# Attention outputs divided by row sums from a ones column, with other hand-overs in the causal loops

## The reference, cut to what matters

```
L1:  S = (mixed q) k^T ; A = softmax(S) ; A = instance_norm(A over 256x256) * gamma + beta ; out = A v ; out @ projW + projb
L2:  S = q k^T / 4, causal ; A = softmax(S) ; out = A v ; t + out @ w_proj
L3:  the same with biases on q, k, v and on the output projection
```

## Time and profile before

| | before |
|---|---|
| median of 3 runs | 975.96 us (975.36 to 980.0) |
| the profiled execution | 974.61 us |
| its span | 972.6 us |
| mean granted clock of TensorE, of full speed | 0.923 |
| busy in the span: PE, weight loads, DVE, ACT, POOL | 83%, 65%, 79%, 65%, 20% |
| loop of l = 1 | about 104 to 326 us |
| loops of l = 2 and l = 3 | about 396 to 538 us, 653 to 796 us |

### The profile page before, as it was taken

How to read it: one execution, slowest core, us unless ns; L and a number is a source line. 1 busy time by engine, 2 the same in 40 slices (tenths; PEclk the granted TensorE clock), 3 DMA queues, 4 the chain that set the end, 5 groups by cost and what they waited for, 6 DMA issues and landing times.

```text
span 972.6 us, 19124 instructions
## 1 busy us (share of the span) xinstructions
PE 808.0 (83%) x5550; PEld 630.5 (65%) x5550; DVE 772.7 (79%) x2166; ACT 632.9 (65%) x1931; POOL 192.6 (20%) x234
## 2 busy tenths in 40 slices
PE   0876698889988755899999486559999997999997
PEld 0762576667766653678887356438778877677775
DVE  7327799999999835699999869938999994688886
ACT  0211587777877513689888564248889874688885
POOL 9001423443234110000000000010000010134344
PEclk9997899999999967799999798779999995799999
DMA  5000000000000091466666200035666650313130
GB/s 184 1 0 1 1 1 0 0 0 0 0 0 0 10 121 28 76 93 97 90 87 83 31 1 1 0 62 83 84 97 96 88 75 0 69 41 82 41 82 17
DMA packets 54355, 44.30 MB, mean 46 GB/s; under 512 B 28592, under 2 KB 42544, under 8 KB 54192
## 3 DMA queue, kind: packets, MB, share of 16 engines
q1 hardware_dynamic: 53872, 42.30, 27.9%
q0 software_dynamic: 448, 1.57, 0.6%
HBM read 12.33 MB, written 3.21 MB: 16 GB/s over the span
## 4 chain that ended last, share of the span: by engine, by line
PE 44%; DVE 12%; DMA 3%; issue 1%; ACT 1%; SPq 1%; POOL 0%; POOLq 0%; DVEq 0%; ACTq 0%
PE ps L839 7%; PE ps L850 6%; PE ps L720 6%; PE ps L624 6%; PE ps L670 5%; PE ps L661 3%; PE ps L626 3%; DVE chst L910 2%; DMA qk<-lo 2%; DVE on L929 2%; PE ps L551 1%; PE ps L634 1%; PE ps L635 1%; PE ps L647 1%; PE ps L826 1%
## 5 line engine op out<-in xcount | busy, mean ns | idle before, releaser
L419 ACT ACTIVATE ee<-ps,nmax 128x128 f32<-128x128 f32 (+1 forms) x588 | 249.5, 443 | 11.7 <-DVE nmax L990 9.9
L1031 DVE TENSOR_SCALAR ee<-ee,rrec 128x128 f32<-128x128 f32 (+1 forms) x588 | 174.8, 360 | 5.2
L720 PE MATMUL ps<-w,ee 128*128 128x128 f32 x960 | 137.0, 279 | 19.9 <-DVE ee L1031 19.9
L406 ACT ACTIVATE big<-ps 128x384 f32<-128x384 f32 (+1 forms) x224 | 113.5, 538 | 40.0 <-PE ps L720 39.4
L720 PEld LDWEIGHTS ps<-w,ee 128*128 128x128 f32 x960 | 103.9, 141 | 45.4 <-DVE ee L1031 35.6
L419 ACT ACTIVATION_READ_ACCUMULATOR ee<-ps,nmax 128x1 f32 x588 | 124.2, 211 | 0.0
L990 DVE TENSOR_REDUCE nmax<-ps 128x2 f32<-128x256 f32 x200 | 101.1, 545 | 18.0 <-PE ps L626 18.0
L624 PE MATMUL ps<-qk 128*128 128x128 f32 (+1 forms) x400 | 103.7, 348 | 13.4 <-DMA qk<-lo 10.8
L296 POOL TENSOR_TENSOR big<-qs,w 96x256 f32<-96x256 f32 x108 | 78.8, 761 | 144.4 <-ACT qs L429 144.4
L1234 DVE TENSOR_TENSOR hhl<-ee,hhl 128x512 fp32r<-128x512 f32 x96 | 81.7, 858 | 27.9 <-ACT hhl L525 26.2
L624 PEld LDWEIGHTS ps<-qk 128*128 128x128 f32 x400 | 79.8, 207 | 31.7 <-issue 17.9
(11 more groups left out here) (224 smaller groups left out, 1365.5 us busy)
## 6 DMA issues: line engine op xcount, KB each, us to landing
qk<-hi SPq DMA_DIRECT2D x36, 192.0 KB, 3.7
qk<-hi SPq DMA_DIRECT2D x72, 96.0 KB, 3.8
qk<-lo SPq DMA_DIRECT2D x36, 192.0 KB, 4.8
qk<-lo SPq DMA_DIRECT2D x72, 96.0 KB, 4.6
big<-moe_gate SPq DMA_DIRECT2D x8, 768.0 KB, 6.9
w<-w_in SPq DMA_DIRECT2D x1, 1831.5 KB, 12.9
xc<-x_in SPq DMA_DIRECT2D x4, 384.0 KB, 5.7
l_mix<-on SPq DMA_DIRECT2D x8, 192.0 KB, 6.6
```

What stands on the lines that cost most here:

```text
L406: nc.scalar.activation(et[:, h, 0:w], ps[:, 4 + hh, 0:w], ACT.Copy).then_inc(own(l, f"et{hh}"), 1)
L419: last = nc.scalar.activation(ee[:, ke, hh, qc, 0:w], src, ACT.Exp, bias=nmax[:, kp, hh, qc:qc + 1], accum_out=rsum[:, kp, hh, qc:qc + 1])
L720: last = nc.tensor.transpose(ps[:, 4 + hh, b * P:(b + 1) * P], ee[:, u, hh, qc, tc * P:(tc + 1) * P], ident)
L1031: last = V.tensor_scalar(v, v, rrec[:, kp, hh, qc:qc + 1], None, ALU.mult)
```

## The change

Four things are done at once.

1. Row sums. `normalise`, the accumulators of the exponentials and the sums of squares are gone. The values carry a column of ones, so that `weigh_values` gives the row sums with the outputs; the transposed outputs are then divided (`normalise_outputs`). In l = 1 the squares come from `bn_stats` of the undivided exponentials, put together behind the loop. Transposes wait for the exponentials themselves.
2. Causal outputs. They are transposed at u = 0, divided at u = 1, transposed back, copied by ACT (`oc`) and projected at u = 2 into bank 7, where before one step at u = 1 projected them in bank 6.
3. Causal queries and keys. Even heads stand in rows 0 to 63 of `qk`, odd heads in rows 64 to 127; a product reads 64 rows. `stack` issues each copy as two DMAs of 48 partitions: twelve for an image. `project_qk` moves ahead of the transposes of u = 0. The causal mask is added by one instruction of 256 columns for each head, not two of 128.
4. Order of ACT and DVE in the causal loops: both copies of probabilities of u = 0 are DVE's, with `keys` between them; `queries` stands right behind the output copy. `w1hl` gets a buffer of its own and is made behind the loop of l = 1, not behind that of l = 3.

```diff
@@ stack (SP)
                         for t, a0, a1 in moves:
-                            sp.dma_start(qk[t * HD:(t + 1) * HD, par, :, a0:a1, :].bitcast(F32),
-                                         part[:, a0:a1, :].bitcast(F32)).then_inc(own(l, "stacked"), 16)
+                            for hh in range(2):
+                                r0 = hh * 4 * HD + t * HD
+                                sp.dma_start(qk[r0:r0 + HD, par, :, a0:a1, :].bitcast(F32),
+                                             part[hh * (C // 2):(hh + 1) * (C // 2), a0:a1, :].bitcast(F32)).then_inc(own(l, "stacked"), 16)
@@ ACT, loop
+                        if l > 1 and u == 2:
+                            outputs_by_channel(l, i - 1)
                         exps(l, k + 1, (j + 1) % 2, (u + 1) % 3)
                         if u == 0:
                             outputs_to_sbuf(l, i - 1)
...
+                        if l > 1 and u == 0:
+                            queries(l, i + 2, par)
                         if l == 1 or u == 1:
                             copy_probs(l, k, 2 * u, 0)
-                        copy_probs(l, k, 2 * u + 1, 1)
-                        if l == 1 and u == 2:
...
+                        if l == 1 or u != 0:
+                            copy_probs(l, k, 2 * u + 1, 1)
@@ score_unit, causal
-                            mm(ps[:, 2 * kp + hh, qc * N:qc * N + w], qk[:, par, h, 0, qc * P:(qc + 1) * P], qk[:, par, h, 1, 0:w],
-                               start=True, stop=False)
-                            last = mm(ps[:, 2 * kp + hh, qc * N + qc * P:qc * N + (qc + 1) * P], identb[:, :], maskb[:, :], start=False, stop=True)
+                            r0 = hh * 4 * HD
+                            mm(ps[:, 2 * kp + hh, qc * N:qc * N + w], qk[r0:r0 + 4 * HD, par, u, 0, qc * P:(qc + 1) * P],
+                               qk[r0:r0 + 4 * HD, par, u, 1, 0:w], start=(qc == 0), stop=False)
+                    for hh in range(2):
+                        diag = ps[:, 2 * kp + hh, :].rearrange("p (b t) -> p b t", t=P)[:, 0::3, :]
+                        last = mm(diag, identb[:, :], mid_dim(maskb[:, :], 1, TPI), start=False, stop=True)
@@ PE, loop
+                        if l > 1 and u == 0:
+                            pe.wait_ge(sg("causal_added"), i + (LOOP_ADDS["added"] if l == 3 else 0) + START)
+                            project_qk(l, i + 2, par)
                         for hh in range(2):
-                            pe.wait_ge(*upto(l, "norm", 2 * k + (hh + 1)))
+                            if l > 1 and u == 2 and hh == 1:
+                                pe.wait_ge(*upto(l, "v_sb", i + 2))
+                                project_outputs(l, i - 1)
+                            pe.wait_ge(*upto(l, "exp", 2 * k + (hh + 1)))
...
@@ DVE
+            def normalise_outputs(l, i):
+                dve.wait_ge(*upto(l, "oq", i + 2))
+                src = ps[:, 6, 0:4 * C].rearrange("p (q h d) -> p q h d", q=TPI, d=2 * HD)
...
+                V.reciprocal(rec, src[:, :, :, HD]).then_inc(own(l, "orec"), 1)
+                dve.wait_ge(*upto(l, "orec", i + 2))
+                for q in range(TPI):
...
+                    last = V.tensor_tensor(dst.rearrange("p (h d) -> p h d", d=HD), src[:, q, :, 0:HD], last_dim(rec[:, q, :], HD), ALU.mult)
+                last.then_inc(own(l, "on" if l > 1 else "added"), 1)
@@ DVE, loop
+                        if l > 1 and u == 1:
+                            normalise_outputs(l, i - 1)
                         maxima(l, k + 2, j % 2)
...
+                        if l > 1 and u == 0:
+                            copy_probs(0)
+                            keys(l, i + 2)
+                            copy_probs(1)
+                        if l > 1 and u == 1:
+                            values(l, i + 1, npar)
+                        if l > 1 and u == 2:
+                            copy_probs(0)
+                            add_outputs(l, i - 1)
                         if l == 1:
-                            dve.wait_ge(sg("l1_norm"), 2 * k + 2)
...
+                            dve.wait_ge(sg("l1_exp"), 2 * k + 2)
+                            for hh in range(2):
+                                for q in range(TPI):
+                                    last = V.bn_stats(est[:, par, q, 2 * u + hh, :], ee[:, u, hh, q, :])
...
-                        normalise(l, k + 1, (j + 1) % 2, (u + 1) % 3)
...
@@ DVE, behind the loop of l = 1
+                    V.tensor_tensor(e4[:, :, :, 0], e4[:, :, :, 1], e4[:, :, :, 1], ALU.mult)
+                    link(V.tensor_tensor(r2, r1, r1, ALU.mult))
+                    link(V.scalar_tensor_tensor(out=e4[:, :, :, 0], in0=e4[:, :, :, 0], scalar=float(N // 2), in1=e4[:, :, :, 2], op0=ALU.mult, op1=ALU.add))
+                    link(V.tensor_tensor(e4[:, :, 0, 0], e4[:, :, 0, 0], e4[:, :, 1, 0], ALU.add))
+                    link(V.tensor_tensor(e4[:, :, 0, 0], e4[:, :, 0, 0], r2, ALU.mult))
+                    V.tensor_tensor(ssqa[:, :, :], e5[:, :, 0, :, 0, 0], e5[:, :, 1, :, 0, 0], ALU.add).then_inc(sg("l1_ssqa"), 1)
```

More of the change, by code:

```diff
@@ L418, in exps @@
                         src = ps[:, 2 * kp + hh, qc * N:qc * N + w]
[L419 to L420 removed]
+                        last = nc.scalar.activation(ee[:, ke, hh, qc, 0:w], src, ACT.Exp, bias=nmax[:, kp, hh, qc:qc + 1])
                     last.then_inc(own(l, "exp"), 1)
@@ L439, in outputs_to_sbuf, with outputs_by_channel @@
                 nc.scalar.activation(ots[0:C, :, :], ps[0:C, 6, :].rearrange("p (a t) -> p a t", a=2), ACT.Copy).then_inc(own(l, "ot"), 1)
+            def outputs_by_channel(l, i):
+                act.wait_ge(*upto(l, "oc_ps", i + 2))
+                nc.scalar.activation(oc[0:C, :], ps[0:C, 6, 0:N], ACT.Copy).then_inc(own(l, "oc"), 1)
             for l in (1, 2, 3):
@@ L1010, in add_outputs @@
             def add_outputs(l, i):
                 dve.wait_ge(*upto(l, "out_ps", i + 2))
-                if l == 1:
-                    for q in range(TPI):
-                        src = ps[:, 6, q * 2 * C:(q + 1) * 2 * C].rearrange("p (h d) -> p h d", d=2 * HD)[:, :, 0:HD]
-                        dst = on1[:, q, i + 1, :] if isinstance(i, int) else on1[:, q, bass.ds(i + 1, 1), :].rearrange("p a c -> p (a c)")
-                        last = V.tensor_copy(dst.rearrange("p (h d) -> p h d", d=HD), src)
-                else:
-                    tv = tok_all[:, bass.ds(i * TPI + TPI, TPI), :]
-                    last = V.tensor_tensor(tv, ps[:, 6, 0:TPI * C].rearrange("p (t c) -> p t c", c=C), tv, ALU.add)
@@ L1021, in add_outputs @@
-                last.then_inc(own(l, "added"), 1)
-            def normalise(l, k, kp, ke):
-                dve.wait_ge(*upto(l, "exp", 2 * k + 2))
-                V.reciprocal(rrec[:, kp, :, :], rsum[:, kp, :, :]).then_inc(own(l, "rec"), 1)
-                dve.wait_ge(*upto(l, "rec", k + 1))
-                for hh in range(2):
-                    for qc in range(TPI):
-                        v = ee[:, ke, hh, qc, 0:scores_cols(l, qc)]
-                        last = V.tensor_scalar(v, v, rrec[:, kp, hh, qc:qc + 1], None, ALU.mult)
-                    last.then_inc(own(l, "norm"), 1)
+                tv = tok_all[:, bass.ds(i * TPI + TPI, TPI), :]
@@ L1034, in _ @@
+                V.tensor_tensor(tv, ps[:, 7, 0:TPI * C].rearrange("p (t c) -> p t c", c=C), tv, ALU.add).then_inc(own(l, "added"), 1)
             for l in (1, 2, 3):
@@ L1052, in _ @@
                 keys(l, 1)
-                normalise(l, 0, 0, 0)
                 with dve.Fori(0, B // 2) as it:
@@ new lines, in _ @@
+                        if l == 1:
+                            dve.wait_ge(sg("l1_exp"), 2 * k + 2)
+                            for hh in range(2):
+                                for q in range(TPI):
+                                    last = V.bn_stats(est[:, par, q, 2 * u + hh, :], ee[:, u, hh, q, :])
+                            last.then_inc(sg("l1_est"), 1)
+                            if u == 2:
+                                dve.wait_ge(sg("l1_est"), TR0 + k + 1)
+                                V.tensor_copy(esta[:, bass.ds(i, 1)].rearrange("p a q h s -> p (a q h s)"),
+                                              est[:, par].rearrange("p q h s -> p (q h s)")).then_inc(sg("l1_esta"), 1)
@@ L1251, in get @@
         return np.asarray(inputs[name])
-    def heads_apart(w, bias=None):
-        out = np.zeros((P, 2, C), w.dtype)
-        out[:C].reshape(3, 2 * HD, 2, C)[:, :HD] = w.reshape(2, 3, HD, C).transpose(1, 2, 0, 3)
-        if bias is not None:
-            out[ONE, 0] = bias
-        return out
     def with_bias(w, bias):
```

159 lines of the change are left out of this document (87 added, 72 removed).

## The result

| | before | after |
|---|---|---|
| median of the runs side by side | 977.81 us (4 runs) | 994.66 us (991.95 to 997.23, 4 runs) |
| ratio, 95% interval | | 1.0173 [1.0131, 1.0215] |
| the profiled execution, its span | 974.61, 972.6 us | 993.85, 991.9 us |
| mean granted clock of TensorE | 0.923 | 0.908 |
| one image in the loop of l = 1 | 13.50 us | 11.81 us |

What follows compares the result with a forecast made beforehand. Bounds: PE's wait for DVE in l = 1; PE and the circle of `hi` together in the causal loops. 974.6 - 29.6 + 2.4 + 2 x (27.0 + 1.9 + 2.1) = 1009.4, forecast 1010 us, range 951 to 1036.

Steps and rivals of the forecast that it cites:

- circle of `hi`: Causal loops: from one `hi` through issuing and landing of its image's copies to the next; forecast 10.5 us.
- slower at 0.68: Whole kernel: the chance of 0.68 given to the change making it slower, against 0.27 for faster.
- Wait before the transposes, l = 1: Loop of l = 1: PE's wait for DVE's normalisation goes, 16 images x 1.85 = -29.6 us.
- Behind the loop of l = 1: After the l = 1 loop: six small DVE instructions before the sum over partitions add 2.4 us.
- clock falls: Rival, causal loops: idle PE drops to the lower clock, periods some 13 us, 80 us more, 1090; chance 5%.
- 0.62 us an issue: Causal loops: a copy of 48 partitions costs SP as much to issue as before, 0.62 us a step.
- half a copy, half an issue: Rival, causal loops: issuing 48 partitions costs under 0.45 us, so the kernel is faster, 953 to 960 us; chance 25%.
- Landing 3.1 us: Causal loops: an image's last small copy lands 1.2 + 0.5 + 1.4 = 3.1 us after its issue.
- the halves land no sooner: Causal loops: by the skill, 48 KB pieces land like 96 KB ones; circle 11.2 us, sum 22 us higher.
- The end of each causal layer: From output copy to last add of l = 2 and 3: 2.2 us becomes about 4.3, +2.1 each.
- The bare circle at the start: Start of each causal layer, no other work in the way: `hi` to `hi` from 8.62 to 10.5 us, +1.9.
- PE's own work: Causal loops: rearranged products may win or lose some tenths of 8.70 us, hidden while the circle is longer.

Runs made afterwards that it cites:

- tiny: Changed kernel with all twelve copies moving only a quarter of their columns (first quarter of the tokens): 988.79 us.
- b12: Kernel before, each of its six copies an image split in two by tokens, nothing else changed: 1018.5 us, ratio 1.0425.
- six: Changed kernel with six copies an image, each of 96 partitions written to every fourth partition: 945.53 us, ratio 0.9673.
- l1only: Kernel before with only the l = 1 part of the change; causal loops keep `normalise` and six copies: 957.03 us, ratio 0.979.
- vsum: Changed kernel with the 32 value sums behind l = 1 put ahead of the sum of squares: 993.48 us, ratio 1.0171.
- six_et1_vsum: `six` with DVE's second copy of probabilities ahead of `lo` at u = 0, and value sums ahead of the sum of squares: 933.25 us.

## Why the prediction was right

The forecast was 1010 us from a longer circle of `hi`, slower at 0.68; measured 994.7, slower, by that mechanism. The closeness of the number is in part luck: one term was 24 us too high, and two others missed by 7 us the other way. Step by step:

- *Wait before the transposes, l = 1: -29.6.* Measured -25.2 in the loop. Another -1.3 stands ahead of it, for a reason that was not tried. No wait for DVE stands before the transposes any more. The 24.6 us of the earlier trace rows are the wait of PE's weight loads; its products waited 16.3 us there, 1.2 an image. The rest of the 1.69 an image is busy time of PE, from 12.3 us an image (165.7 of 182) to 11.7. The period is 11.81 for the 11.7 forecast, with PE busy for 183.9 of 185 us (105 to 290), so that PE itself is what comes next, as foreseen. Only fifteen periods got shorter (15 x 1.69 = 25.4): the first image's, which fills the pipeline, did not.
- *Behind the loop of l = 1: +2.4.* Mis-sized: +6.6. The two 384-element instructions with strided operands took 0.68 and 0.68, not half of a 1.03 pair; the chain is 3.1 us. The larger part was not in the sum: behind PE's 4.00 us of idleness the clock was 0.50, and the products took 3.3 us more. The rival "clock falls" was put into the causal loops, where it did not come (1.00 from 403 to 540 us in l = 2) and not here, where it did. At the start of l = 2, where PE waits for the first copies, the clock is 0.50 from 373 to 383 us; the kernel before has such a stretch too.
- *0.62 us an issue.* Right: 0.63 a step (3.78 us for six), 592 ns each. The rival "half a copy, half an issue" is false; `tiny` extends that to 12 KB, a sixteenth of 192. The price follows the number of DMAs.
- *Landing 3.1 us.* Mis-sized: 2.1 us. This is the largest error: the period came to 9.70 for 10.5. The prediction added 1.2 us before the first packet and 1.4 behind the last, 2.6 in all; `tiny`, with 12 KB a copy, lands in 1.8 altogether. With the measured period in its place the sum is 1009.4 - 2 x 15 x 0.8 = 985.4; the miss behind l = 1 (+4.2) and the smaller gain up to there (+3.1) bring it to 992.7, beside the 993.85 of the profiled execution.
- *Where the Trainium skill was weighed* (DMA: Bandwidth & Descriptors, Rules for kernel authors: two transfers to disjoint partition halves serialise). Taken as "the halves land no sooner", which gave a circle of 11.2 us, it did not hold: 2.1 us where that circle had 3.8. That has nothing to do with partition halves, for `b12`, which splits by tokens, lands in 2.1 us too. Its advice, one transfer for two, held for another reason, the issue: `six` is 49 us faster.
- *The end of each causal layer: +2.1.* Right: from the last `hi` to the last add 8.16 us became 10.23 in l = 2 and 8.18 became 10.25 in l = 3, +2.1 each; the chain from the output copy is 4.0 us for the 4.3 forecast. The bare circle at the start, forecast at +1.9: 8.62 to 9.87 in l = 2 (362.94 to 372.81), +1.2, and 8.72 to 11.24 in l = 3, +2.5.
- *PE's own work, "some tenths".* Right: `six`, which PE bounds, has 8.47 for 8.70, and it was hidden in the changed kernel, as was the order of the two copies on DVE (8.23).

The three losses and gains add up from kernel to kernel: 977 to 957 by l = 1, to 945.5 by the causal part with six copies, to 994.7 by splitting them.

## What to carry to other kernels

Count the DMA issues of a loop as work of the engine that issues them. For the copies within SBUF of these kernels, n x 0.6 us plus one landing is a circle while the source buffer is single, and halving the bytes or the partitions of each changed only the landing. Before splitting a copy for a better layout, look for a layout that one copy can reach (a partition stride did here). Two buffers took the landing out of the circle, but the starts of the layers still paid for every issue.

## What the runs showed of the hardware beyond that

**The rows that a copy writes, and how close the copies follow, go with the load on the DMA engines.** The same 768 KB an image, in as many packets (54,355 and 54,354 in the whole execution), kept the DMA engines busy for 0.62 of the time in the kernel before (copies into 16 adjacent partitions) and for 0.33 in `six` (every fourth of 128), both from 410 to 500 us. The last copy of `six` lands 2.3 us after its issue for 4.7. GB/s in 40 slices around one image's copies, first the kernel before (slices of 0.2 us from 455), then `six` (0.15 us from 462):

```profile
GB/s 0 0 0 0 0 0 154 266 246 282 154 174 108 118 108 149 200 113 133 195 102 154 164 149 82 102 102 118 108 103 169 133 46 5 0 0 0 0 0 0
```

```profile
GB/s 0 0 0 0 0 0 0 0 0 14 177 164 218 273 260 273 273 266 96 157 246 198 62 123 191 205 287 266 253 273 232 116 137 260 212 14 0 0 0 0
```

The first is at 102 to 118 in ten of its last 24 slices, the second returns to 250 to 287. The Trainium skill (SBUF — State Buffer, Door 1: The DMA port swizzle) says that 16 adjacent partitions reach 4 of 16 ports, some 109 GB/s, and that partitions spread over the array reach them all. Those ten slices agree; the first 0.8 us of the kernel before, at 154 to 282, and eleven of the later slices, at 133 to 200, are above that figure, so the agreement is partial, and several copies were in flight at a time. The changed kernel and `b12` write to 16 adjacent partitions too, and their engines are busy for only 0.28 and 0.29. They issue an image's 768 KB over 7.5 us and not over 3.7, an estimate of some 105 GB/s for some 210. So the adjacent rows fill the engines where the copies follow closely; with twelve issues they don't. The prediction worked out its landing from full engines and did not ask what filled them.

**POOL and DVE slowed each other in l = 1.** POOL's mixing of one image takes 3.47 us for 4.46, though its instructions are the same. It is so in `l1only` too, where DVE has `bn_stats` beside it and no more products of two operands, and ACT has lost its accumulators and one square. DVE's side shows in the timeline of the kernel before, first `normalise` beside the mixing, then without it:

```profile
198.28 4.46 POOL L296 TENSOR_TENSOR big<-qs,w 96x256 f32<-96x256 f32 x6 [8.63 <-ACT qs L429]
...
201.16 2.13 DVE L1031 TENSOR_SCALAR ee<-ee,rrec 128x256 f32<-128x256 f32 x4
...
206.10 1.14 DVE L1031 TENSOR_SCALAR ee<-ee,rrec 128x256 f32<-128x256 f32 x4
```

The same four instructions take 2.13 us beside the mixing and 1.14 behind it, and a square of two equal operands (L1068) takes up to 1.09 us beside it and 0.68 otherwise. Part of the wait that the change removed from PE was of this kind. Whether it was DVE's squares or its divisions that held POOL up was not tried.

**TensorE after an idle time.** In the changed kernel the 32 products behind 4.00 us of idleness took 7.04 us, in `vsum` behind 0.98 us 3.78; the ratio is nearly that of the clock's two levels, 2.4 and 1.2 GHz, and the granted clock was 0.50 and 1.00. In `six_et1_vsum`, with the same order as `vsum`, they took 5.37 us in the profiled execution: the clock was 1.00 up to 302 us and 0.51 from there to 305.3, with PE busy all the time. So the short gap alone does not decide it.
